# A third wait ahead of the GpSimd scatters of a two-layer graph network on one Trainium2 core

## The chip, the core and the metric

The kernel runs on one core of one Trainium2 chip. The metric is the device time of one execution in microseconds, the median of three runs.

## What is computed

The input is a graph of 6250 nodes with 128 features and 100000 edges, sorted by `dst`. Two layers follow each other, each ended by a residual addition and a layer norm:

```python
# layer 0
h = silu(concat(x[src], x[dst], radial(edge_weight)) @ Wm1 + bm1)
h = silu(h @ Wm2 + bm2);  messages = h @ Wm3 + bm3
out = segment_sum(messages, dst)
u = silu(concat(x, out) @ Wu1 + bu1) @ Wu2 + bu2
x = layernorm(x + silu(u @ Wi1 + bi1) @ Wi2 + bi2)
# layer 1, with xt = logmap0(x)
att = sigmoid(concat(xt[src], xt[dst], edge_attr) @ att_w + att_b)
agg  = segment_sum(xt[src] * att, src)
mean_src = segment_sum(edge_attr, src) / count(src)
mean_dst = segment_sum(edge_attr, dst) / count(dst)
x = layernorm(x + proj(expmap0(xt + agg + mean_src + mean_dst)))
```

`edge_attr` is 100000 rows of 128 floats. Summing its rows by `dst` is easy, since the edges come in that order; summing them by `src` needs them moved, and that is what the changed line is about.

## The kernel before

The edges are cut into M = 196 chunks of 512 edges (four tiles of 128). Five engines run their own instruction streams, written out tick by tick, and meet through semaphores. A stream is in order: an instruction that waits holds everything behind it on its engine.

**Edges of layer 0** (ticks -6 to 203). For each chunk GpSimd (POOL) issues four indirect gathers of projected node rows (L1060), which may run at most six chunks ahead of TensorE (`h1p`). TensorE turns them and multiplies (L1284 to L1324), ScalarE applies SiLU, VectorE builds one-hot matrices and adds each chunk's sum into an accumulator. All 784 gathers stand in POOL's stream ahead of the first scatter.

**Rows of layer 1** (row tick r = t - 190, so they overlap the last edges). Row chunk i passes these steps, with `row` a ring of NE = 8 slots:

- SyncE (SP) loads 512 edge rows into slot i % 8 (`row_load`, L893 to L896), three ticks before use. It first waits until the scatters of chunk i-8 have landed (`sc`) and until TensorE has summed chunk i-8 (`rp`).
- VectorE builds the window one-hot `od2` (L978) and the products for the attention (L981 to L996); ScalarE sums them into one more column of the slot (L944, or L949 and L952) and raises `lb`.
- One tick later TensorE sums the chunk by `dst` into a window of 78 nodes: four float matmuls, which are eight rows of the profile (`rows_pe`, L1010). The last raises `rp`, so `rp` counts the chunks summed. VectorE adds the window to `acce` (L970).
- POOL scatters the slot's rows to a table in HBM, grouped by `src` (`rows_pool`, L928 to L935): four indirect DMAs per chunk. It waits for the chunk's index (`idx`) and for `lb`.

SP's stream at a row tick r is: load of row chunk r+3, then for the later chunks the three look-up loads of chunk r+4 (L1428), then the loads of the units (below) of tick r+2 (L1414). All stand behind the wait of the row load.

**Units of layer 1** (row ticks 68 to 201). The table is read back in 189 units of up to six tiles (L1414), and each is summed by `src` with one-hot matmuls (VectorE L1534, TensorE L1651, VectorE L1557 or L1559). The edges are split in five groups (chunks 0 to 61, 62 to 112, 113 to 151, 152 to 178, 179 to 195); units of a group are loaded only when all scatters of the group have landed. Units 0 to 48 also need an attention sum on ScalarE (L1476). Units 172 to 188 belong to the last group, which ends with the last scatter.

After row tick 199 TensorE transposes the sums by `dst` (L1639), ScalarE scales them (L1483), the last units follow, and VectorE and ScalarE finish the nodes.

Of the kernel before, what the change touches and what calls it, by code (L numbers as in the profile page):

```python
# [7 lines left out]
M = 196  # L8
# [18 lines left out]
CAP = [q[1] * P for q in GROUPS]  # L27
FILL = 4
NCST = 264
STAGE = 9400  # L30


# [4 lines left out]
def group_of(m):  # L37
    return next(i for i in range(NG) if m <= LAST[i])
# [39 lines left out]
def limits():  # L78

    low = [2 * P * sum(1 for k in NDONE[:-2] if k <= m) for m in range(M)]  # L80
    high = [FREE - W if m < NFREE else 2 * EARLY * P - W if m < NEARLY else TOP for m in range(M)]
    return low, high
# [107 lines left out]
def gnn_kernel(nc, A, out):  # L190
# [10 lines left out]
    with ctx:  # L201

        def sb(name, shape, dt=f32):
            return ctx.enter_context(nc.sbuf_tensor(name, shape, dt))
# [7 lines left out]
        def take(reg, shape, dt=f32):  # L212
            n = 1
            for k in shape:
                n *= k
            return reg.take(shape, None if dt == f32 else dt, n // 2 if dt == bf16 else n)

        s = {n: ctx.enter_context(nc.semaphore(n)) for n in PRO + LAYER + NODES + ROWS + REST}
# [10 lines left out]

        cst = sb("cst", [P, NCST])  # L230
        ident, iota = cst[:, 0:128], cst[:, 128:256]
# [65 lines left out]
        sp1 = take(ring, [1])  # L297
        ring.off = STAGE
        stq = [take(ring, [4, H]) for _ in range(13)]
# [26 lines left out]
        def prologue_sp(e):  # L326
# [18 lines left out]
            for q in range(13):  # L345
# [4 lines left out]
                if q == 0:  # L350
                    SP.dma_start(lims.rearrange("o a m -> o (a m)"), A["consts"][0:1, NCST:NCST + 2 * M]).then_inc(s["lim"], 16)
                    e.wait_ge(s["c1"], 5)
# [29 lines left out]
        def prologue_act(e):  # L382
            S.dma_start(cst[:, :], A["consts"][:, 0:NCST]).then_inc(s["cst"], 16)
            e.wait_ge(s["z0"], 1)
            S.copy(sp1[:, 0:1], zerof[:, 0:1])
            for j in range(2):
                S.dma_start(x_sb[:, 12 * j:12 * j + 12, :], A["x"][12 * j * P:(12 * j + 12) * P, :].rearrange(
                    "(b p) f -> p b f", p=P)).then_inc(s[f"pt{j}"], 16)
            for t in range(14):
                q = t  # L390
                if q < 13:
                    nq = min(4, NB - 4 * q)
                    e.wait_ge(s["xt"], q + 1)
                    S.copy(xT[:, 4 * q * P:(4 * q + nq) * P], banks[5 + q % 2][:, 0:nq * P]).then_inc(s["xtc"], 1)
                q = t - 1
                if q >= 0:
                    nq = min(4, NB - 4 * q)
                    e.wait_ge(s["pp"], q + 1)
                    S.copy(stp[q][:, 0:nq, :].rearrange("p i f -> p (i f)"), banks[(0, 7)[q % 2]][:, 0:nq * P]).then_inc(s["pv"], 1)
            for q in range(13):  # L400
                nq = min(4, NB - 4 * q)
                e.wait_ge(s["qp"], q + 1)
                S.copy(stq[q][:, 0:nq, :].rearrange("p i f -> p (i f)"), banks[1 + q % 4][:, 0:nq * P]).then_inc(s["qv"], 1)
# [311 lines left out]
        rest0 = ring.off  # L715
        assert 13 * 4 * H + 8 * M + 1 <= rest0 <= STAGE
        od2 = [take(ring, [4, W]) for _ in range(NO2)]
        prod = [take(ring, [4, H + W]) for _ in range(NPR)]
        bwin = [take(ring, [W]) for _ in range(NWN)]
        row = [take(ring, [4, RC]) for _ in range(NE)]  # L720
        assert ring.off >= STAGE + 13 * 4 * H
        pat = take(ring, [FILL * RC])
# [204 lines left out]
        def rows_pool(e, i):  # L927
            e.wait_ge(s["idx"], i + 1)  # L928
            e.wait_ge(s["idxe"], 4)
            e.wait_ge(s["zf"], 16 * len(FILLS))  # L930
            e.wait_ge(s["lb"], i + 1)
            for n in range(4):
                G.indirect_dma_start(  # L933
                    out=gtab[group_of(i)][:, :], out_offset=bass.IndirectOffsetOnAxis(ap=idx[:, n, i:i + 1], axis=0),
                    in_=row[i % NE][:, n, :], in_offset=None).then_inc(s[f"sc{i % NE}"], 16)  # L935
# [112 lines left out]
        def layer_pool(e):  # L1048
            e.wait_ge(s["tp"], 13 * 16)
            e.wait_ge(s["r2"], 3)  # L1050
            e.wait_ge(s["b3"], 48)
            e.wait_ge(s["rb"], 1)
            e.wait_ge(s["c1"], 5)
            e.wait_ge(s["r3"], 5)
            for t in TICKS:
                i = chunk(t, 0)
                if i is not None:
                    e.wait_ge(s["h1p"], i + 1 - NGP)
                    for n in range(4):
                        G.indirect_dma_start(  # L1060
                            out=gp[i % NGP][:, n, :], out_offset=None, in_=ptab[:, :],
                            in_offset=bass.IndirectOffsetOnAxis(ap=gis[:, n, i:i + 1], axis=0)).then_inc(s[f"gp{i % NGP}"], 16)
            for i in range(RE):
                rows_pool(e, i)
# [392 lines left out]
        def rest_pool(e):  # L1457
            for i in range(RE, M):
                rows_pool(e, i)
# [614 lines left out]
def consts():  # L2074

    import numpy as np
    c = np.zeros((128, NCST + 2 * M), np.float32)
    p = np.arange(128)
# [12 lines left out]
    c[:, 263] = 1.0  # L2091
    c[0, NCST:] = np.array(limits(), np.float32).ravel()
    return c
# [18 lines left out]
```

## Time and profile before

| what | value |
|---|---|
| median of the runs | 2124.54 us (2124.5 to 2126.67, 3 runs) |
| profiled execution, first to last instruction | 2669.9 us |
| busy: PE, DVE, ACT, POOL | 66%, 63%, 51%, 56% of that span |
| gathers L1060 and scatters L933 on POOL | 784 each |
| first gather, first scatter, last scatter | 32.6, 1237.3, 2546.1 us |

The profiled execution is one execution with the profiler on; no other time of it is given than its span. The timed runs carry no profiler and are 545 us shorter. PE is TensorE's matmuls, DVE is VectorE, ACT is ScalarE, POOL is GpSimd, SP is SyncE. Idle time with the releaser "issue" is time in which the profile shows nothing that the engine waited for.

### The profile page before, as it was taken

How to read it: one execution, taken by the hardware profiler on the slowest of the kernel's cores; microseconds unless marked ns; L12 is line 12 of the kernel's file. 1: busy time of each engine (PE TensorE's matmuls, PEld its weight loads, DVE VectorE, ACT ScalarE, POOL GpSimd, SP SyncE). 2: the span in 40 equal slices, each digit the busy share in tenths (PEclk: the TensorE clock that was granted, in tenths of full speed). 3: DMA queues.
4: the chain of work that ended last, by engine and by line, in shares of the span. 5: the costliest groups of instructions: out<-in, count | busy, mean ns of one | idle time of the engine just before them, and what ended most of it. 6: DMA issues, size and time to landing. Idle time of an engine off the chain costs nothing.

```text
span 2669.9 us, 41647 instructions
## 1 busy us (share of the span) xinstructions
PE 1766.1 (66%) x11127; PEld 1530.4 (57%) x11127; DVE 1679.0 (63%) x5490; ACT 1361.0 (51%) x3965; POOL 1498.9 (56%) x1572
## 2 busy tenths in 40 slices
PE   5677777777878787776643244777775666576770
PEld 5466665655666666565533233677665656576660
DVE  5666666666666677776535334788765555466668
ACT  3666665665666666875425333666643233233224
POOL 3566666665666666655566665566555455555510
PEclk8788888898888778997755556677777677777795
DMA  7465655654333233333433335566555455455541
GB/s 192 122 148 124 150 131 130 148 133 111 88 84 86 84 86 85 87 83 103 133 89 100 87 105 140 160 187 186 171 155 151 147 154 152 142 168 167 172 136 49
DMA packets 337140, 341.98 MB, mean 128 GB/s; under 512 B 67402, under 2 KB 266948, under 8 KB 336898
## 3 DMA queue, kind: packets, MB, share of 16 engines
q1 hardware_dynamic: 283474, 233.47, 33.7%
q0 software_dynamic: 50176, 104.07, 13.2%
q10 hardware_dynamic: 3248, 1.71, 0.3%
q8 instruction: 93, 1.52, 0.2%
q14 instruction: 149, 1.22, 0.1%
HBM read 246.14 MB, written 90.15 MB: 126 GB/s over the span
## 4 chain that ended last, share of the span: by engine, by line
PE 30%; DVE 20%; issue 17%; another core or an unknown queue 15%; ACT 11%; DVEq 3%; SPq 0%; DMA 0%; ACTq 0%
PE bank L1651 8%; PE bank L1010 5%; PE bank L1630 4%; PE bank L1311 3%; DVEq L758 3%; PE bank L1284 3%; PE bank L1324 3%; DVE rt L987 2%; ACT L1093 2%; ACT L779 2%; ACT ring L1093 1%; PE bank L1320 1%; DVE ring L1184 1%; DVE ring L978 1%
## 5 line engine op out<-in xcount | busy, mean ns | idle before, releaser
L933 POOL DMA_INDIRECT gtab<-ring,idx x784 | 753.9, 962 | 556.3 <-ACT ring L952 238.9
L1060 POOL DMA_INDIRECT ra<-ptab,gis x784 | 744.9, 950 | 491.6 <-issue 199.7
L1010 PE MATMUL bank<-ring 128*128 128x78 f32 x1568 | 299.9, 341 | 284.0 <-issue 220.9
L949 ACT ACTIVATE rt<-rt 128x254 f32<-128x254 f32 x536 | 215.4, 403 | 470.7 <-DVE rt L989 347.6
L1010 PEld LDWEIGHTS bank<-ring 128*128 128x128 f32 x1568 | 278.0, 258 | 306.6 <-issue 251.0
L1284 PEld LDWEIGHTS bank<-ring 128*128 128x128 f32 x1568 | 232.9, 215 | 175.9 <-issue 153.8
L1073 ACT ACTIVATE ring<-bank 128x512 f32<-128x512 f32 x196 | 116.3, 594 | 395.3 <-remote 349.0
L1284 PE MATMUL bank<-ring 128*128 128x78 f32 x1568 | 238.1, 293 | 103.4 <-issue 86.4
L1651 PE MATMUL bank<-ring 128*128 128x130 f32 x1312 | 230.7, 332 | 86.5 <-issue 67.2
L1630 PE MATMUL bank<-rt 128*128 128x126 f32 x1072 | 196.6, 328 | 108.0 <-issue 73.8
L1311 PEld LDWEIGHTS bank<-wm,ring 128*128 128x128 f32 x1568 | 250.7, 228 | 25.5 <-issue 10.9
L1651 PEld LDWEIGHTS bank<-ring 128*128 128x128 f32 x1312 | 207.0, 238 | 100.5 <-issue 79.8
L1311 PE MATMUL bank<-wm,ring 128*128 128x128 f32 x1568 | 256.7, 316 | 11.5 <-issue 7.6
L1630 PEld LDWEIGHTS bank<-rt 128*128 128x128 f32 x1072 | 175.9, 240 | 114.1 <-issue 113.9
L1169 DVE TENSOR_TENSOR ra<-ra,bank 128x78 f32 x196 | 46.4, 237 | 234.3 <-issue 107.4
L1559 DVE TENSOR_TENSOR ra<-ra,bank 128x130 f32<-128x130 f32 (+2 forms) x140 | 47.4, 339 | 198.8 <-remote 156.4
L1324 PE MATMUL bank<-ra,ring 128*128 128x512 f32 x264 | 164.2, 709 | 7.5 <-issue 5.1
L944 ACT ACTIVATE ring<-ring 128x206 f32<-128x206 f32 x248 | 90.2, 366 | 149.2 <-issue 81.2
L1320 PE MATMUL bank<-cst,ra 128*128 128x128 f32 x784 | 147.7, 316 | 17.5 <-issue 17.3
L987 DVE SCALAR_TENSOR_TENSOR rt<-cst,rt,bank 128x125 f32<-128x125 f32 x536 | 147.7, 339 | 0.0
L1093 ACT ACTIVATE ring<-bank,bcol 128x512 f32<-128x512 f32 x196 | 134.6, 687 | 19.1 <-remote 15.1
L970 DVE TENSOR_TENSOR ra<-ra,bank 128x78 f32 x196 | 45.7, 233 | 152.4 <-remote 79.7
(274 smaller groups left out, 3817.3 us busy)
## 6 DMA issues: line engine op xcount, KB each, us to landing
ring<-in_edge_attr SPq DMA_DIRECT2D x196, 256.0 KB
ring<-gtab SPq DMA_DIRECT2D x89, 393.0 KB
gtab<-ring SPq DMA_DIRECT2D x36, 687.8 KB
ra<-in_edge_weight SPq DMA_DIRECT2D x132, 128.0 KB
ring<-gtab SPq DMA_DIRECT2D x49, 327.5 KB
ring<-reld SPq DMA_DIRECT2D x196, 78.0 KB
ring<-gtab SPq DMA_DIRECT2D x49, 262.0 KB
ra<-ptab,gis POOLq DMA_INDIRECT x784
```

Source lines behind the costliest of these rows:

```text
L933: G.indirect_dma_start(out=gtab[group_of(i)][:, :], out_offset=bass.IndirectOffsetOnAxis(ap=idx[:, n, i:i + 1], axis=0), in_=row[i % NE][: ...
L949: k = S.activation(prl[i % NPR][:, n, :], prl[i % NPR][:, n, :], ACT.Identity, accum_out=lgs[i % 2][:, n:n + 1])
L987: V.scalar_tensor_tensor(out=v[:, n, H:H + NM], in0=iota[:, 0:NM], scalar=srcm[:, n, i:i + 1], in1=bk[:, n, 0:NM], op0=ALU.is_equal, op1=A ...
L1010: k = T.matmul(bk[:, 256:256 + W], row[i % NE][:, n, 0:H], od2[i % NO2][:, n, :], start=(first and n == 0), stop=(n == 3), skip_group_chec ...
L1060: G.indirect_dma_start(out=gp[i % NGP][:, n, :], out_offset=None, in_=ptab[:, :], in_offset=bass.IndirectOffsetOnAxis(ap=gis[:, n, i:i + 1 ...
L1093: S.activation(h1[i % 2], banks[(1, 5)[i % 2]][:, :], ACT.Silu, bias=bcol[:, 3:4]).then_inc(s["h1"], 1)
L1284: k = T.matmul(small_bank(t)[:, 0:W], val[i % NVAL][:, n, :], ohd[i % NOD][:, n, :], start=(n == 0), stop=(n == 3), skip_group_check=True)
L1311: k = T.matmul(bk[:, n * P:(n + 1) * P], h1[i % 2][:, n * P:(n + 1) * P], wm2[:, :], start=False, stop=True, skip_group_check=True)
L1320: T.matmul(bk[:, n * P:(n + 1) * P], v[:, n, :], ident, start=(n == 0), stop=False, is_transpose=True, skip_group_check=True)
L1324: T.matmul(bk[:, :], qw[i % NQW], rad[i % NRD], start=False, stop=True, skip_group_check=True).then_inc(s["h1p"], 1)
L1630: k = T.matmul(banks[(1, 2)[i % 2]][:, n * P:n * P + NM + 1], lkf[i % 2][:, n * P:(n + 1) * P], tw[i % NLK][:, 0:NM + 1], start=(n == 0), ...
L1651: k = T.matmul(bk[:, j * (H + 2):(j + 1) * (H + 2)], coh1[(u - 4) % NCO][:, j * nk + n, :], ct[(u - 4) % NCT][:, j * nk + n, 0:H + 2], sta ...
```

## The change

POOL waits once more before the four scatters of chunk i: until TensorE has summed min(i + 3, 196) chunks, that is chunks i, i+1 and i+2. For chunks 194 and 195 the count was already waited for at chunk 193, so 194 of the 196 chunks get the new wait.

```diff
@@ -27,6 +27,7 @@
 FILL = 4
 NCST = 264
+AHEAD = 3
 STAGE = 9400
@@ -929,6 +930,7 @@
             e.wait_ge(s["idxe"], 4)
             e.wait_ge(s["zf"], 16 * len(FILLS))
             e.wait_ge(s["lb"], i + 1)
+            e.wait_ge(s["rp"], min(i + AHEAD, M))
             for n in range(4):
                 G.indirect_dma_start(
```

No instruction moves, on any engine; the line numbers behind the edits grow by one or two. POOL's stream, in the middle of the scatters, of the kernel before (the table's size stands behind its name, and x3 are three more of the same chunk):

```order
L933 DMA gtab<-ring,idx 51456x131 [waits lb,idx]
L933 DMA gtab<-ring,idx 51456x131 x3
L933 DMA gtab<-ring,idx 51456x131 [waits lb,idx]
L933 DMA gtab<-ring,idx 51456x131 x3
L933 DMA gtab<-ring,idx 51456x131 [waits lb,idx]
```

The same place in the changed kernel:

```order
L935 DMA gtab<-ring,idx 51456x131 [waits rp,lb,idx]
L935 DMA gtab<-ring,idx 51456x131 x3
L935 DMA gtab<-ring,idx 51456x131 [waits rp,lb,idx]
L935 DMA gtab<-ring,idx 51456x131 x3
L935 DMA gtab<-ring,idx 51456x131 [waits rp,lb,idx]
```

The first scatter of each chunk names a third semaphore, and nothing else differs.

## Rows read from the trace of the kernel before

**Rows 1.** The page's head and first part: the span, and busy us and shares of the engines

```profile
span 2669.9 us, 41647 instructions
PE 1766.1 (66%) x11127; PEld 1530.4 (57%) x11127; DVE 1679.0 (63%) x5490; ACT 1361.0 (51%) x3965; POOL 1498.9 (56%) x1572
```

**Rows 2.** The page's groups: busy us, mean ns of one, idle before and its releaser

```profile
L933 POOL DMA_INDIRECT gtab<-ring,idx x784 | 753.9, 962 | 556.3 <-ACT ring L952 238.9
L1060 POOL DMA_INDIRECT ra<-ptab,gis x784 | 744.9, 950 | 491.6 <-issue 199.7
```

**Rows 3.** POOL in order of time: start, us, what, idle before; first gathers, last scatters

```profile
32.55 1.11 POOL L1060 DMA_INDIRECT ra<-ptab,gis  x1 [32.10 <-DMA ptab<-ring]
...
81.28 0.99 POOL L1060 DMA_INDIRECT ra<-ptab,gis  x1 [18.32 <-PE bank L1324]
82.58 0.94 POOL L1060 DMA_INDIRECT ra<-ptab,gis  x1 [0.30 <-issue]
...
2531.47 0.96 POOL L933 DMA_INDIRECT gtab<-ring,idx  x1 [6.22 <-ACT ring L952]
...
2542.34 0.96 POOL L933 DMA_INDIRECT gtab<-ring,idx  x1 [0.30 <-issue]
...
2546.14 0.96 POOL L933 DMA_INDIRECT gtab<-ring,idx  x1 [0.30 <-issue]
```

**Rows 4.** PE in order of time, 2196 to 2209 us: single matmuls far apart

```profile
2198.91 0.36 PE L1651 MATMUL bank<-ring 128*128 128x130 f32 x1 [1.05 <-issue]
2200.33 0.27 PE L1651 MATMUL bank<-ring 128*128 128x130 f32 x1 [1.06 <-issue]
...
2208.99 1.85 PE L1010 MATMUL bank<-ring 128*128 128x78 f32 x8
```

**Rows 5.** Busy us (count) of PE, PEld, DVE, ACT, POOL in four stretches; clock, DMA

```profile
300.00:1000.00 700.00, 544.23 (x3568) 438.62 (x3568) 470.53 (x1620) 440.43 (x599) 435.65 (x460) 0.85 0.44 110
1242.40:1602.60 360.20, 152.30 (x732) 137.62 (x733) 154.29 (x513) 138.98 (x620) 222.78 (x232) 0.55 0.37 100
1694.00:1901.00 207.00, 149.02 (x900) 141.43 (x900) 165.59 (x453) 132.66 (x744) 124.24 (x130) 0.76 0.63 177
1954.00:2547.00 593.00, 399.55 (x2452) 374.00 (x2453) 335.07 (x982) 177.60 (x863) 319.47 (x332) 0.74 0.53 154
```

**Rows 6.** POOL in order of time: first scatters of chunks 40, 41, 43; last of 41

```profile
1491.88 0.96 POOL L933 DMA_INDIRECT gtab<-ring,idx  x1 [0.30 <-issue]
...
1499.49 0.96 POOL L933 DMA_INDIRECT gtab<-ring,idx  x1 [2.87 <-remote]
...
1503.28 0.96 POOL L933 DMA_INDIRECT gtab<-ring,idx  x1 [0.31 <-issue]
...
1509.59 0.96 POOL L933 DMA_INDIRECT gtab<-ring,idx  x1 [0.30 <-issue]
```

**Rows 7.** PE in order of time: sums by dst of chunks 42 and 45

```profile
1489.15 1.97 PE L1010 MATMUL bank<-ring 128*128 128x78 f32 x8 [0.77 <-issue]
...
1504.13 1.96 PE L1010 MATMUL bank<-ring 128*128 128x78 f32 x8 [0.43 <-issue]
```

**Rows 8.** SP in order of time: the row load of chunk 49

```profile
1508.31 0.38 SPq L896 DMA_DIRECT2D ring<-in_edge_attr  x1
```

**Rows 9.** DVE in order of time: one tick with a unit's attention, first groups of two ticks

```profile
1801.61 0.23 DVE L970 TENSOR_TENSOR ra<-ra,bank 128x78 f32 x1 [0.54 <-issue]
...
1806.69 0.23 DVE L970 TENSOR_TENSOR ra<-ra,bank 128x78 f32 x1
```

**Rows 10.** The tail, PE then DVE in order of time, and the chain's longest ACT piece

```profile
2541.38 1.01 PE L1010 MATMUL bank<-ring 128*128 128x78 f32 x8
...
2554.66 11.45 ACT ra L1483 x44
...
2570.99 0.95 DVE L1534 TENSOR_TENSOR gis<-bank,ring 128x768 f32<-128x768 f32 x1
```

**Rows 11.** The tail: SP's unit loads from 2567.88, and DVE's first use of that one

```profile
2567.88 4.40 SPq L1414 DMA_DIRECT2D ring<-gtab  x4
...
2573.40 0.95 DVE L1534 TENSOR_TENSOR ring<-bank,ring 128x768 f32<-128x768 f32 x1
```

## The prediction

> **What bounds the kernel now.** I read the page first, then the groups, then the engines in order of time. The page says that no engine is busy for more than 66% of 2669.9 us [rows 1], and that POOL's two groups have nearly the same price: 0.950 us per gather and 0.962 us per scatter, 784 of each [rows 2]. In order of time an indirect DMA is followed by the next after 0.30 us even where nothing is waited for [rows 3]. So a gather takes 1.25 us of POOL's stream and a scatter 1.262 us, and a chunk of four takes 5.0 or 5.05 us.
>
> Next the stretches [rows 5]. I divide by the chunks in each, POOL's count over four:
> - edges (115 chunks): PE 4.73, DVE 4.09, POOL 3.79 busy and 5.0 with its gaps, of 6.09 us;
> - stage A, rows alone (58 chunks): PE 2.63, DVE 2.66, ACT 2.40, POOL 5.05, of 6.21;
> - stage B, rows and units with attention (32.5 chunks): DVE 5.10, PE 4.59, ACT 4.08, POOL 5.05, of 6.37;
> - stage C, rows and plain units (83 chunks): PE 4.81, DVE 4.04, ACT 2.14, POOL 5.05, of 7.14.
>
> No sum per chunk reaches the stretch's own pace. What fills the difference is seen on PE: after a dense run come single matmuls 1.4 us apart, with idle time that nothing explains, until it is dense again [rows 4]. I take these to belong to the profiled execution, because the timed runs are 545 us shorter. Laying POOL's stream end to end gives a check: 32.55 us before the first gather, 784 x 1.25 = 980.0, the one long wait of 18.3 at the start, 784 x 1.262 = 989.4, and 2669.9 - 2547.1 = 122.8 after the last scatter [rows 1 to 3]. That is **2143 us, 0.9% above the median of 2124.54**. A kernel whose POOL stream alone adds up to its time has next to no idle POOL in the runs. So I read the runs as bound by POOL in the edges, in A and in C, and balanced between POOL (5.05) and DVE (5.10) in B.
>
> **The change, step by step.** The edit touches only POOL's stream. It adds a condition to 194 scatters and no DMA, load or matmul. The condition itself is priced at nothing: chunks already open with two waits, and the gap at such a scatter, 0.30 us where nothing is late, is the gap inside a chunk [rows 3, 6]. Held to both sides it costs 0 to 194 x 0.30 = 58 us (a whole gap for every wait). I take 0, since two waits show none, and give 58 us no part of the range: it would need a third wait to cost what two together do not.
>
> What the wait can cost is POOL idle until TensorE has summed chunk i+2.
> - *Where POOL is behind*, it costs nothing. The trace has such a place in A: chunk 40 is scattered from 1491.88, and the sum of chunk 42 ends at 1489.15 + 1.97 = 1491.12; chunk 43 goes at 1509.59, the sum of 45 ended at 1506.09, 3.5 us before [rows 6, 7]. With POOL the bound the ring of eight slots decides how far. The last scatter of chunk 41 leaves POOL at 1504.24 and the load into its slot is issued at 1508.31 [rows 6, 8], so a landing costs at most 4.1 us. From the first scatter of chunk i to the sum of i+8 I count 5.05 + 4.1, about 4 for the load and two to three for VectorE and TensorE: some 17 us. Chunk i+6 is scattered 30 us after chunk i, so the sum of i+8 is there 13 us early. The margin is **13 us**.
> - *Start.* POOL's gathers stand ahead of scatter 0, so the rows pipeline runs ahead of it up to the ring's eight slots. Scatters start a few chunks late with their sums made: 0 us.
> - *B.* DVE's tick is 1806.69 - 1801.61 = 5.08 us [rows 9], POOL's 5.05. POOL catches up by 0.03 us in each of 49 ticks, 1.5 us of the 13: 0 us.
> - *C.* DVE 4.04 against POOL 5.05: POOL falls behind again, 0 us.
> - *End.* In the profile POOL is not behind here. The sum of chunk 195 ends at 2541.38 + 1.01 = 2542.39; chunk 193's scatters began at 2531.47 and 195's at 2542.34 [rows 3, 10]. Now the twelve scatters of 193 to 195 all start after 2542.39, and the last ends 15.1 us later at 2557.5 instead of 2547.1: **10.4 us later**. Behind it wait the units of the last group. Their first use on VectorE is at 2570.99, because ScalarE's scaling of the sums by dst holds TensorE for 11.45 us [rows 10]. With 4.1 to land and 5.5 for the unit's load (2567.88 to 2573.40, the closest load and use in the tail [rows 11]), they are there at 2567.1. So it is covered; without that cover it is 10.4. In the runs, with POOL behind, the sums are done before and nothing is late.
>
> The sum is 0 us of POOL idle in the runs, and 0 to 4 on the profiled span of 2669.9 us, where covers are thinner. The time stays 2124.5.
>
> One rule speaks against the change. The row shows only that a landing costs up to 4.1 us past POOL's last scatter [rows 6, 8]. The Trainium skill, DMA: Bandwidth & Descriptors, Rules for kernel authors, says to issue a DMA early and wait for it late; here each scatter is issued later, up to 2.5 ticks. By the rule the deferral is lost time, the 12.7 us of rival 1 and a time of 2137; by the row it is lost only where POOL is not behind, and the sum stays 0. The same page, Anatomy of one DMA, puts a fixed cost of about 2.0 us on a DMA; by that, an estimate, the margin would be 15 us and the sum the same.
>
> **The rivals.**
> 1. *Slower: POOL catches up in B and then pays.* If a B tick in the runs is above 5.05 + 13/49 = 5.32 us, the margin is gone before B ends. The wait then opens holes that the old order filled, up to 2.5 ticks of 5.08, **12.7 us**, and C, being POOL's, never gives them back: up to 2137. For it: DVE's 5.08 has its own gap of 0.54 in front, and look-up loads are late now and then. Against it: TensorE's 4.59 and ScalarE's 4.08 leave DVE alone near the line [rows 5].
> 2. *Slower: SP is held in C.* SP waits for the scatters of chunk i before it issues the loads that stand behind (row, look-ups, units), and in a kernel not bound by POOL that closes a loop of four ticks: 5.05 + 4.1 after the sum of i+2, 5.5 for the loads, about 2.5 to the next sum, 17.2 us, so no tick under 4.3. Against DVE's 4.04 it would be 84 x 0.26 = 22 us, 2146. It needs a POOL faster than 4.3 us per chunk in the runs, against rows 2 and 3.
> 3. *Faster.* Scatters held back leave the DMA engines (busy share 0.53 to 0.63 in B and C [rows 5]) to the loads for a while. If the runs are waiting for loads rather than POOL, the price is at most rival 2's, the other way; I put it at half, 11 us, 2113. Nothing of it counts while POOL is the bound.
> 4. *The runs are like the profile*, POOL idle for a fifth of A to C. Then only the end changes, 0 to 4 us: up to 2128. It falls in "same".
>
> **How the numbers follow.** A measurement of this kernel can tell 0.2%, 4.2 us. Forecast, no POOL idle: 0.56, of which 0.02 for a wait that costs after all. Rival 4: 0.08. Rival 1: 0.22, of which 0.19 costs more than 4.2 us. Rival 2: 0.07. Rival 3: 0.07. Faster by over 0.2%: 0.07. Slower: 0.19 + 0.07 + 0.02 = 0.28. The rest, 0.65, within 0.2%. The time is the likeliest, 2124.5. The range takes in rival 1 whole (2137) and a little of rival 2, up to 2139, and of rival 3 a part, down to 2119; outside lie most of rivals 2 and 3, 0.12.
>
> **What would show it.** In the profile after, POOL's scatters name TensorE's L1010 as releaser, for a few hundred microseconds of idle time that was put down to ScalarE before, and the first scatter of a chunk stands right behind the third sum, in B and C some 12 us later than now. The last scatter starts about 10 us later against the last L1010. The groups' counts and mean durations stay. The span stays near 2670 us. Wrong would be: the median moved by over 4 us; a longer idle of VectorE in front of L1534 or L1525 with loads as releaser (rival 2); or a DVE tick in B above 5.3 us (rival 1).

## The result and the profile after

The kernel before takes 2124.5 us (2121.14 to 2126.67, 5 runs), the changed one **2132.41 us** (2131.18 to 2136.2, 5 runs): a ratio of 1.0039, 95% interval 1.0028 to 1.005, or 7.9 us slower. The prediction had 2124.5, no difference. The time lies in its range of 2119 to 2139, on the side that was given 0.28.

One thing must be known to read what follows. The experiments ran in sets, each of several kernels that run on one chip in turn with the kernel before, and every set fell in one of two conditions. In the **first condition** the kernel before takes 2120 to 2125 us. In the **second condition** all kernels of the set are longer, and the kernel before takes 2674 to 2703 us. The profile of before that the prediction read (2669.9 us) is of the second condition; its three timed runs and the result above are of the first. One chip showed both, in different sets. Each run below stands against the kernel before of its own set.

The page of the changed kernel, its head and its two POOL groups, against [rows 1, 2]:

```profile
span 2133.5 us, 41647 instructions
PE 1544.3 (72%) x11127; PEld 1322.7 (62%) x11127; DVE 1677.7 (79%) x5490; ACT 1360.0 (64%) x3965; POOL 1505.0 (71%) x1572
...
L1062 POOL DMA_INDIRECT ra<-ptab,gis x784 | 748.2, 954 | 272.5 <-issue 235.2
L935 POOL DMA_INDIRECT gtab<-ring,idx x784 | 756.6, 965 | 248.2 <-issue 220.0
```

POOL's busy time is that of before within 7 us, and its idle time in front of gathers and scatters is 521 us where it was 1048. Of the 521, 455 (235.2 and 220.0) are put down to "issue", the 0.30 us gaps. That is the reading that the forecast assumed for the runs: a stream of POOL with next to no holes. Before and after stand in different conditions here, so this fall isn't the effect of the change.

Four stretches of the changed kernel (busy us and count of PE, PEld, DVE, ACT, POOL; then clock, DMA share, GB/s), one in each of the prediction's stages: edges, A, B, C, against [rows 5]:

```profile
300.00:1000.00 700.00, 580.85 (x4384) 461.96 (x4384) 587.47 (x2113) 562.10 (x823) 530.25 (x557) 0.97 0.49 124
1100.00:1330.00 230.00, 98.12 (x414) 89.08 (x414) 114.51 (x367) 96.90 (x483) 174.57 (x183) 0.51 0.41 117
1366.00:1568.00 202.00, 142.19 (x1109) 129.81 (x1108) 199.05 (x553) 162.33 (x912) 153.34 (x160) 1.00 0.83 225
1609.00:1956.00 347.00, 268.95 (x2004) 260.13 (x2004) 275.77 (x813) 142.28 (x684) 264.14 (x273) 0.89 0.78 220
```

By POOL's count over four these are 139.25, 45.75, 40 and 68.25 chunks, so 5.03, 5.03, 5.05 and 5.08 us per chunk, where the prediction had 6.09 to 7.14 from [rows 5]. In every stretch the pace is POOL's. In B, VectorE is busy for 199 of 202 us: balanced, as predicted.

POOL in order of time (start, us, what, idle before and its releaser), against [rows 3, 6]: the first gather, the first scatters of chunks 0 to 6, of 40 (and the last of it), of 193, and the last of all. Of the later gathers only the one at 64.83 us is idle for over 0.5 us before it, for 1.92:

```profile
32.46 1.11 POOL L1062 DMA_INDIRECT ra<-ptab,gis  x1 [32.01 <-DMA ptab<-ring]
...
1021.41 0.99 POOL L935 DMA_INDIRECT gtab<-ring,idx  x1 [0.30 <-issue]
...
1026.77 0.96 POOL L935 DMA_INDIRECT gtab<-ring,idx  x1 [0.56 <-issue]
...
1033.73 0.96 POOL L935 DMA_INDIRECT gtab<-ring,idx  x1 [2.20 <-PE bank L1012]
...
1041.94 0.96 POOL L935 DMA_INDIRECT gtab<-ring,idx  x1 [3.47 <-PE bank L1012]
...
1048.88 0.96 POOL L935 DMA_INDIRECT gtab<-ring,idx  x1 [2.17 <-PE bank L1012]
...
1055.10 0.96 POOL L935 DMA_INDIRECT gtab<-ring,idx  x1 [1.46 <-PE bank L1012]
...
1061.10 0.96 POOL L935 DMA_INDIRECT gtab<-ring,idx  x1 [1.25 <-PE bank L1012]
...
1233.77 0.96 POOL L935 DMA_INDIRECT gtab<-ring,idx  x1 [0.30 <-issue]
...
1237.57 0.96 POOL L935 DMA_INDIRECT gtab<-ring,idx  x1 [0.30 <-issue]
...
2011.01 0.96 POOL L935 DMA_INDIRECT gtab<-ring,idx  x1 [0.30 <-issue]
...
2024.92 0.96 POOL L935 DMA_INDIRECT gtab<-ring,idx  x1 [0.30 <-issue]
```

Over the plain gap of 0.30 the six idle times are 0.26 + 1.90 + 3.17 + 1.87 + 1.16 + 0.95 = **9.3 us**, and of the other scatters none waits over 0.5 us. Laid end to end: 32.5 before the first gather, 989.0 to the first scatter, 1004.5 to the end of the last, 107.6 behind it, 2133.5 us; without the 9.3 it is 2124.2, near the time of before. It can't be taken as nearer than a few us: the profiled execution is the longest of the five (2136.2 us), and its span is 2.7 us shorter than its time. The sums by dst on TensorE say why POOL waits. Chunks 2 to 8, then 42 and 195:

```profile
1016.78 1.12 PE L1012 MATMUL bank<-ring 128*128 128x78 f32 x8 [2.36 <-DVE ring L980]
...
1024.87 1.12 PE L1012 MATMUL bank<-ring 128*128 128x78 f32 x8 [1.22 <-DVE ring L980]
...
1031.82 1.12 PE L1012 MATMUL bank<-ring 128*128 128x78 f32 x8 [1.32 <-DVE ring L980]
...
1039.16 2.00 PE L1012 MATMUL bank<-ring 128*128 128x78 f32 x8 [2.34 <-DVE ring L980]
...
1046.97 1.12 PE L1012 MATMUL bank<-ring 128*128 128x78 f32 x8
...
1053.19 1.12 PE L1012 MATMUL bank<-ring 128*128 128x78 f32 x8 [1.42 <-DVE ring L980]
...
1059.20 1.12 PE L1012 MATMUL bank<-ring 128*128 128x78 f32 x8 [0.97 <-DVE ring L980]
...
1213.23 1.97 PE L1012 MATMUL bank<-ring 128*128 128x78 f32 x8 [3.01 <-DMA ring<-in_edge_attr]
...
2004.32 1.01 PE L1012 MATMUL bank<-ring 128*128 128x78 f32 x8
```

The seven sums from 1016.78 to 1059.20 start one every 7.1 us, while POOL asks for one in 5.06. In this stretch both engines have the last edges to do as well: TensorE is busy for 34.83 of the 42.40 us, VectorE for 31.73, and before six of the sums TensorE waits for VectorE. The next two sums end at 1064.28 and 1068.95 us, each 4 to 5 us after the one before. When the first scatter could go, at 1021.4, three sums were made. Against a POOL that went on at 5.06 us, each later one was further behind until chunk 8. This lateness is called the debt below.

### The profile page after: what moved, and what is told of

It is laid out like the page before. It is cut to its first block, busy times and chain, and to the rows that moved or that the text cites. A ratio compares the mean times of both kernels' runs of the same rounds, so it can differ in the third digit from the quotient of the medians.

```text
span 2133.5 us, 41647 instructions
## 1 busy us (share of the span) xinstructions
PE 1544.3 (72%) x11127; PEld 1322.7 (62%) x11127; DVE 1677.7 (79%) x5490; ACT 1360.0 (64%) x3965; POOL 1505.0 (71%) x1572
## 4 chain that ended last, share of the span: by engine, by line
DVE 34%; POOL 25%; issue 15%; DMA 8%; PE 7%; DVEq 7%; ACT 2%; SPq 1%; POOLq 0%; ACTq 0%
POOL gtab L935 16%; POOL ra L1062 10%; DVEq L759 6%; DVE ring L1186 4%; DVE ring L1196 3%; DMA gtab<-ring,idx 3%; DVE ring L1201 2%; PE bank L1653 2%; DVE bank L1210 2%; DVE rt L989 2%; DMA ring<-btab 2%; DMA rt<-bval 2%; DVE ring L1191 2%; DVE ring L1207 2%; DVE ring L1188 2%
## 5 line engine op out<-in xcount | busy, mean ns | idle before, releaser
L1062 POOL DMA_INDIRECT ra<-ptab,gis x784 | 748.2, 954 | 272.5 <-issue 235.2
L1012 PE MATMUL bank<-ring 128*128 128x78 f32 x1568 | 260.2, 323 | 133.3 <-DMA ring<-in_edge_attr 94.4
L1012 PEld LDWEIGHTS bank<-ring 128*128 128x128 f32 x1568 | 246.3, 239 | 144.3 <-issue 116.3
L1286 PEld LDWEIGHTS bank<-ring 128*128 128x128 f32 x1568 | 198.8, 195 | 147.2 <-DVE ra L1171 129.0
L1286 PE MATMUL bank<-ring 128*128 128x78 f32 x1568 | 210.5, 278 | 67.1 <-DVE ring L1178 61.6
L1632 PE MATMUL bank<-rt 128*128 128x126 f32 x1072 | 167.1, 305 | 105.4 <-DVE rt L991 91.1
L1653 PE MATMUL bank<-ring 128*128 128x130 f32 x1312 | 183.9, 292 | 56.8 <-DVE ra L1561 43.1
L1313 PEld LDWEIGHTS bank<-wm,ring 128*128 128x128 f32 x1568 | 215.5, 200 | 12.4 <-ACT ring L1095 6.4
L1632 PEld LDWEIGHTS bank<-rt 128*128 128x128 f32 x1072 | 149.3, 215 | 118.1 <-issue 117.9
L1313 PE MATMUL bank<-wm,ring 128*128 128x128 f32 x1568 | 217.6, 284 | 4.9 <-ACT ring L1095 4.9
L1653 PEld LDWEIGHTS bank<-ring 128*128 128x128 f32 x1312 | 165.4, 200 | 66.1 <-DVE ra L1561 47.6
L1171 DVE TENSOR_TENSOR ra<-ra,bank 128x78 f32 x196 | 46.4, 237 | 130.1 <-issue 121.9
L1527 DVE TENSOR_SCALAR rt<-rt,cst 128x512 f32<-128x512 bf16 x134 | 67.5, 504 | 102.0 <-DMA rt<-bval 101.1
L1322 PEld LDWEIGHTS bank<-cst,ra 128*128 128x128 f32 x784 | 95.0, 148 | 62.9 <-DMA ra<-ptab,gis 62.8
```

Of the source, the lines that this page charges most:

```text
L1012: k = T.matmul(bk[:, 256:256 + W], row[i % NE][:, n, 0:H], od2[i % NO2][:, n, :], start=(first and n == 0), stop=(n == 3), skip_group_chec ...
L1062: G.indirect_dma_start(out=gp[i % NGP][:, n, :], out_offset=None, in_=ptab[:, :], in_offset=bass.IndirectOffsetOnAxis(ap=gis[:, n, i:i + 1 ...
L1286: k = T.matmul(small_bank(t)[:, 0:W], val[i % NVAL][:, n, :], ohd[i % NOD][:, n, :], start=(n == 0), stop=(n == 3), skip_group_check=True)
L1313: k = T.matmul(bk[:, n * P:(n + 1) * P], h1[i % 2][:, n * P:(n + 1) * P], wm2[:, :], start=False, stop=True, skip_group_check=True)
L1322: T.matmul(bk[:, n * P:(n + 1) * P], v[:, n, :], ident, start=(n == 0), stop=False, is_transpose=True, skip_group_check=True)
L1632: k = T.matmul(banks[(1, 2)[i % 2]][:, n * P:n * P + NM + 1], lkf[i % 2][:, n * P:(n + 1) * P], tw[i % NLK][:, 0:NM + 1], start=(n == 0), ...
```

## The experiments

Theory (the start theory of the expectations): the whole cost is this debt at the start. Rivals: a cost at every chunk (of the third wait itself, or of loads that come later in B and C), and a cost at the end. The first set also has the kernel before again.

**e1, the wait at chunks 7 and later alone.**

```diff
-            e.wait_ge(s["rp"], min(i + AHEAD, M))
+            if i >= 7:
+                e.wait_ge(s["rp"], min(i + AHEAD, M))
```

> The new wait stands only at chunks 7 and later; chunks 0 to 6 keep the two old waits. Theory (the start pays): the profile of the changed kernel shows POOL idle over its 0.30 us gap only at the scatters of chunks 1 to 6, together 9.3 us; without the wait there, the time is that of the kernel before, 2124.5 us (2121 to 2127), and POOL's scatters of chunks 0 to 6 follow each other every 5.05 us. Rival (the wait costs a little at every chunk, by its own execution or by loads that come later in B and C): the cost is spread over 196 chunks, 189 of them are left, so 2132 us. Rival (half and half, the pipeline downstream loses elsewhere what it gains at the start): between 2127 and 2130.

**e2, the wait at chunks 0 to 6 alone** (`if i < 7:`).

> The new wait stands only at chunks 0 to 6. Theory (the start pays): the whole cost is there, 2132.4 us (2130 to 2135), with POOL idle some 9 us over its gaps at chunks 1 to 6 released by TensorE's bank. Rival (the wait costs at every chunk): the time of the kernel before, 2124.5 us.

**e3, one chunk ahead** (`AHEAD = 2`).

> The scatters of chunk i wait for the sum by dst of chunk i+1 instead of i+2. From the ends of the sums in the profile of the changed kernel (1010.6, 1017.9, 1026.0, 1032.9, 1041.2, 1048.1, 1054.3, 1060.3 for chunks 1 to 8) and a first scatter at 1021.4 with 5.06 us a chunk, chunk i waits for: chunk 1 at 1026.5 none, 2 at 1031.5 until 1032.9 (1.4 us), 3 at 1038.0 until 1041.2 (3.2), 4 at 1046.3 until 1048.1 (1.8), 5 at 1053.2 until 1054.3 (1.1), 6 at 1059.4 until 1060.3 (0.9), 8.4 us, if the sums do not come earlier when the scatters do. That is nearly the cost of the changed kernel, 2124.5 + 8.4 x 0.85 = 2131.6 us. Should the sums come earlier because the scatters do (the unit and row loads stand behind them), the cost is less, about 2 us: 2126.5. Rival (a cost at every chunk whatever it waits for): 2132.4.

**e4, the kernel before, unchanged.**

> The kernel before, unchanged, for a profile of it near the time of its runs. Theory: the span is near 2125 us, not 2670; TensorE has no matmuls 1.4 us apart; POOL has no idle time over its 0.30 us gap at the scatters of chunks 1 to 6, and the sums of chunks 2 to 8 end after the scatters of chunks 0 to 6 begin. Rival (the single matmuls belong to the kernel before and the change has removed them): a span near 2670 us again.

Measured in that set: the kernel before 2702.74 us (2682.73 to 2720.06, 17 runs); e1 2598.93, ratio 0.9603 (0.9558 to 0.9647); e2 2702.33, ratio 0.9994 (0.9963 to 1.0026); e3 2579.31, ratio 0.9536 (0.9492 to 0.958); e4 2690.46. No expectation was made for this condition, and only the span of e4's rival fits (2687.6 us, near 2670 again). Its reason, that the change had removed the single matmuls, doesn't: e3 has the wait, and its TensorE is still idle for 169.2 us in front of L1012 with the releaser "issue". Two things follow. The single matmuls far apart [rows 4] do not belong to a profiled execution, as I had written: here all 17 runs of the kernel before take even longer than that profile. And the wait from chunk 7 on, which costs 0.3% in the first condition (e7 below), takes 4% off in the second (e1). The changed kernel itself was not run in the second.

**e5, the changed kernel again, and e6, three chunks ahead** (`AHEAD = 4`), in one set.

> The changed kernel itself, beside the one before, in the same call as the next run. The first four runs of this study fell on a chip where the kernel before takes 2703 us, TensorE has its single matmuls 0.7 to 1.4 us apart in the profile, and the wait at chunks 7 and later alone took the time down to 2599 us (ratio 0.960), while the wait at chunks 0 to 6 alone left it (0.999). Theory: there are two conditions of the chip with two answers. Where the kernel before takes some 2700 us, the changed kernel takes 2600 us, as with the late wait alone (2590 to 2610). Where it takes 2124, the changed kernel takes 2132. Rival: the 2124 and 2132 of the first result were two different days and the change is faster on every chip: a ratio of 0.96 with a time near 2040.

> The scatters of chunk i wait for the sum by dst of chunk i+3. Where the kernel before takes 2124 us (start theory): from the ends of the sums in the profile of the changed kernel, scatter 0 waits for 1026.0 and scatter 6 for 1064.3, 13 to 15 us at the start; in B the margin of 5.2 us less a tick of 5.06 is nothing and in C 2 to 7 us less 5 costs 0 to 40 us more: 2138 to 2180. The rival that only the start pays: 2138 to 2140. Where it takes 2700 us: the time between the sum of i+3 and the load of the row i+8 closes a loop of five ticks instead of six, about 22 us for scatter, landing, load and sum, 4.4 us per tick against the 6.2 us that the stretches keep there, so no cost: 2590 to 2610.

This set fell in the first condition: before 2121.8 us, e5 2130.03, ratio 1.0034 (1.0021 to 1.0048), 8.2 us, so the result stands. e6 took 2172.53, ratio 1.0254 (1.0236 to 1.0272), 50.7 us, inside the 2138 to 2180 of the margins and not the 2138 to 2140 of a start that alone pays. The waits view of e6 from 1360 us on, in stages B and C (waited for: us in total, times, longest):

```profile
POOL gtab L935 <- PE bank L1012: 38.8, 37, 3.8
```

One more chunk uses up what margin there was in B and C. Over the plain gaps e6's POOL is idle for 49.9 us, and 11.7 of them lie before 1060 us, so some 38 of the 50.7 are lost in B and C.

**e7 to e9 repeat e1 to e3, and e10 is four chunks ahead** (`AHEAD = 5`).

> The new wait at chunks 7 and later alone, again, meant for the condition in which the kernel before takes 2122 us. Start theory: nothing is left of the cost, 2122 (2119 to 2125). Rival (a cost at every chunk): 2130. Where it falls on a chip like that of the first four runs: 2599 against 2703 as before, and the question stays as it was.

> The new wait at chunks 0 to 6 alone, again, meant for the same condition. Start theory: the whole cost, 2130 (2128 to 2133). Rival (a cost at every chunk): 2122.

> One chunk ahead instead of two, again, meant for the same condition. By the ends of the sums in the changed kernel 8.4 us of POOL idle at chunks 2 to 6, and 2129; if the sums come earlier when the scatters do, because row loads stand behind them, about 2 us and 2124.

> The scatters of chunk i wait for the sum of chunk i+4. Three chunks ahead (scatter i behind the sum of i+3) cost 50.7 us over the kernel before, of which the start was put at 13 to 15. Loop theory: scatter i lets the row load of i+8 go (POOL's four scatters 5.06, landing 2 to 3.6, load 4, VectorE and TensorE 2 to 3, 14 to 17 us in all), and scatter i+4 waits for the sum of i+8: a loop over four chunks with 14 to 17 us plus the wait of SP in order, so a tick of 3.7 to 4.3 us by itself, but 5.06 is POOL's; the cost comes from the look-up and unit loads that stand ahead of the row load on SP. From 50.7 at three chunks ahead I expect the margin to be short by another tick in B and C, where the sum came 2 to 7 us before it was asked for at two ahead: another 5 us once and then a tick longer than POOL's, 5.6 to 7.5 us in B and C (131 chunks): 2250 to 2500. Start-only rival: 2143.

The kernel before took 2124.19 us (18 runs); e7 2129.5, ratio 1.0031 (1.0019 to 1.0043); e8 2130.73, 1.003 (1.0019 to 1.0041); e9 2125.24, 1.0005 (0.9996 to 1.0014); e10 2359.24, 1.1108 (1.1093 to 1.1123).

e8 came as expected (2128 to 2133). e7 is a miss: 5.3 us where I expected none. POOL in order of time in e7, the first scatters of chunks 7 and 9:

```profile
1063.07 0.96 POOL L936 DMA_INDIRECT gtab<-ring,idx  x1 [6.24 <-PE bank L1013]
...
1074.13 0.96 POOL L936 DMA_INDIRECT gtab<-ring,idx  x1 [1.25 <-PE bank L1013]
```

The first seven chunks went at POOL's pace, and the debt was asked for whole at chunk 7. So the cost is not a sum over the chunks that wait but about the largest lateness among them: with e8's 6.5 us it would make 11.8, and both waits together cost 8.2 (e5). My cut at 7 was too early for the test.

e9 shows the same from the other side. POOL in order of time, first scatters of chunks 5 to 7:

```profile
1047.81 0.96 POOL L935 DMA_INDIRECT gtab<-ring,idx  x1 [1.32 <-PE bank L1012]
...
1054.12 0.96 POOL L935 DMA_INDIRECT gtab<-ring,idx  x1 [1.52 <-PE bank L1012]
...
1060.12 0.96 POOL L935 DMA_INDIRECT gtab<-ring,idx  x1 [1.26 <-PE bank L1012]
```

One chunk less is 5.06 us of debt less: 3.2 us of idle time over the gaps, and 1.05 on the time, not to be told from none. The 8.4 us that I expected of e9 had set each scatter against a sum one chunk too far on. In all these kernels the time grows by less than POOL's idle time over the gaps: 7.9 for 9.3 us in the changed kernel, 6.5 for 8.0 in e8, 5.3 for 7.6 in e7. No run shows where the 1 to 2 us between them go. e10 fell in the range of the loop theory, 235 us slower. Its waits views, whole run, for POOL and VectorE:

```profile
POOL gtab L935 <- PE bank L1012: 251.2, 101, 8.7
```

```profile
DVE rt L1527 <- DMA rt<-bval: 308.9, 112, 10.1
```

The same wait of VectorE in the changed kernel:

```profile
DVE rt L1527 <- DMA rt<-bval: 101.1, 71, 9.3
```

VectorE waits three times as long for a look-up load, which SP issues behind its wait for the scatters.

**e11 and e13, the wait at chunks 20 and later alone** (`if i >= 20:`), **e12 and e14, a third wait that is met long before**, at every chunk:

```diff
-            e.wait_ge(s["rp"], min(i + AHEAD, M))
+            e.wait_ge(s["rp"], max(i - NE + 1, 1))
```

> The new wait at chunks 20 and later alone. With the wait at 7 and later the time was 2129.5 against 2124.2, and its profile shows POOL idle for 6.24 us at chunk 7 and 1.25 at chunk 9: the debt of the start was paid there, because the sum of chunk 9 was still 7 us late against scatters that follow each other every 5.06 us. From chunk 19 on the sum of i+2 ends 17 us before the scatters of i ask for it in every profile of this condition. Start theory, in its new form (the cost is the largest lateness of a sum over all chunks that wait): nothing, 2124 (2122 to 2126). Rival (a wait costs something in B, C or at the end too): at most 1.0 us was seen at chunk 189, 2125; over that, 2127 to 2129, if what was lost at chunk 7 was not the cause.

> A third wait at all 196 chunks' scatters, but for the sum of chunk i-7 (of chunk 0 at the first ones), which is there long before: the price of the condition alone. Step priced at 0: 2124 (2122 to 2126), and a gap of 0.30 us before each scatter as inside a chunk. Upper end of the range that was written down: 0.30 us for each of 196, 2183. If a met wait costs 10 ns, 2126.

The set fell in the second condition (before 2673.86 us): e11 2568.45, ratio 0.9593 (0.9549 to 0.9637); e12 2673.96, 1.0008 (0.9979 to 1.0037). Both were taken again, with the wait in **C alone** (`if i >= 113:`) and in **A and B alone** (`if 20 <= i < 113:`).

> The wait at chunks 20 and later alone, again. Where the kernel before takes 2124 us: start theory 2124 (2122 to 2126); rival (the wait costs in B, C or at the end) 2127 to 2130. Where it takes 2700: 0.96 of it, as before.

> A third wait at every chunk that is met long before, again: the ratio was 1.0008 [0.9979, 1.0037] where the kernel before took 2674 us. Where it takes 2124: 1.000 (2122 to 2126).

> The wait at chunks 113 and later alone (stage C). Where the kernel before takes 2124 us: 2124; if C or the end costs anything by itself, 2126 to 2129. Where it takes 2700: the profiles of that condition have 7.3 us per chunk in C without the wait and 6.25 with it, so 82 x 1.05 = 86 us, but POOL is also 20 us ahead of TensorE when C begins: 70 to 86 us of the 105 to 120, ratio 0.968 to 0.974. Rival (the gain needs the wait in A and B): 1.00.

> The wait at chunks 20 to 112 alone (A and B). Where the kernel before takes 2124 us: 2124. Where it takes 2700: what is left of the gain, 20 to 40 us, ratio 0.985 to 0.993; the rival has the whole gain, 0.96.

First condition, before 2120.45 us (33 runs): e13 2121.25, ratio **1.0005** (0.9996 to 1.0014); e14 2120.97, 1.0002 (0.9993 to 1.0011); e15 2120.43, 1.0 (0.9991 to 1.0009); e16 2120.96, 1.0002 (0.9993 to 1.0011). A met wait costs nothing that these runs can tell (at most 2.3 us by the interval), and neither does this one from chunk 20 on, in A, B, C or at the end (at most 3.0 us, e13). What is left is the start. In e13's waits view of the whole run there is still TensorE as POOL's releaser, but no wait is longer than the gap:

```profile
POOL gtab L936 <- PE bank L1013: 10.4, 34, 0.3
```

e14 also shows the debt as it lies in the order of before. POOL, first scatters of chunks 0, 6 and 8, then TensorE's sum of chunk 8:

```profile
1017.66 0.98 POOL L935 DMA_INDIRECT gtab<-ring,idx  x1 [0.30 <-issue]
...
1048.01 0.96 POOL L935 DMA_INDIRECT gtab<-ring,idx  x1 [0.30 <-DVE idx L1212]
...
1059.25 0.96 POOL L935 DMA_INDIRECT gtab<-ring,idx  x1 [1.27 <-ACT ring L946]
```

```profile
1055.64 1.12 PE L1012 MATMUL bank<-ring 128*128 128x78 f32 x8 [0.97 <-DVE ring L980]
```

The sum of chunk 8 ends at 1056.76, **8.75 us** after chunk 6 was scattered. From a sum's end to the scatter that it releases e7 has 0.78 us (1061.23 + 1.06 to 1063.07). That makes 9.5, less the 0.97 us over the gap that POOL waits at chunk 8 here for ScalarE, which a later stream would not meet: 8.6 us, against 7.9 and 8.2 measured. That is the largest of four: the first scatter comes earliest in e14 (1017.66 us, in the others 1019.6 to 1021.8). In the profiles of e13, e15 and e16, which have no wait at the start either, the sum of chunk 8 ends 6.2, 4.6 and 6.3 us after chunk 6 is scattered, which makes 5.4 to 7.1 with the 0.78. The debt has the size of the cost, within 3 us.

**e17 and e18 repeat e15 and e16.**

> The wait in C alone, meant for the condition in which the kernel before takes 2700 us: ratio 0.968 to 0.974, C at 6.3 us a chunk instead of 7.3. Rival (the gain needs the wait in A and B): 1.00. Where the kernel before takes 2124: 1.000 again.

> The wait in A and B alone, the same: ratio 0.985 to 0.993, C at 7.3 us a chunk; the rival has 0.96. Where the kernel before takes 2124: 1.000 again.

This set fell in the second condition, before 2679.56 us: C alone 2578.1, ratio 0.9628 (0.958 to 0.9675), A and B alone 2657.17, 0.9937 (0.9901 to 0.9974). C holds nearly the whole gain, even a little more than I gave it. What changes is seen on TensorE in C, 1990 to 2380 us. First e17, the windows row (its columns as above) and TensorE's longest waits. "Issue" is again idle time for which the profile shows no reason:

```profile
1990.00:2380.00 390.00, 278.04 (x1851) 265.06 (x1852) 253.85 (x757) 130.71 (x627) 243.19 (x252) 0.80 0.63 181
```

```profile
PE bank L1654 <- issue: 31.4, 26, 6.2
PE bank L1013 <- issue: 26.1, 32, 1.2
PE bank L1654 <- DVE ra L1562: 25.0, 9, 8.6
PE bank L1633 <- issue: 14.4, 18, 1.8
```

The same of e18, which has no wait in C:

```profile
1990.00:2380.00 390.00, 251.48 (x1534) 233.97 (x1534) 211.86 (x630) 109.06 (x523) 201.06 (x209) 0.72 0.52 149
```

```profile
PE bank L1654 <- issue: 70.1, 55, 5.3
PE bank L1013 <- issue: 39.1, 52, 1.8
PE bank L1654 <- DVE ra L1562: 16.6, 7, 4.6
PE bank L1633 <- issue: 11.6, 19, 1.2
```

With the wait: 63 chunks in 390 us, 6.19 each, of which 71.9 / 63 = 1.14 are such idle time. Without it: 52.25 chunks, 7.46 each, with 120.8 / 52.25 = 2.31. A chunk gains 1.27 us, and on TensorE these are made up so: **1.17 us less** idle time without a visible cause, 0.40 less busy time (4.81 to 4.41, at a granted clock of 0.72 and 0.80), and 0.30 more of the other waits, nearly all for VectorE. In the first condition C has none of the first in this view: e15 from 1610 to 1940 us needs 5.06 us a chunk, at a granted clock of 0.92, and its longest wait is for VectorE:

```profile
1610.00:1940.00 330.00, 246.60 (x1898) 236.79 (x1897) 262.50 (x777) 136.13 (x654) 250.45 (x261) 0.92 0.78 221
```

```profile
PE bank L1654 <- DVE ra L1562: 55.7, 29, 4.0
```

What TensorE stalls on there, and why it stalls less when scatters are held back, stays open. No run here changes that alone. The DMA engines aren't ruled out: over 40 slices of this stretch their traffic swings between 49 and 268 GB/s in e18 and between 146 and 215 in e17.

## Why the prediction was wrong

- **Bound.** Right for the runs: POOL's stream end to end, 5.03 to 5.08 us a chunk in all four stretches of the profile after. The argument for it was right (the sum over POOL's stream against the median), but its 0.9% had luck in it: of the pieces taken from the other condition, the long wait of the gathers is 1.9 us here and not 18.3, and the end behind the last scatter 107.6 and not 122.8, while gathers and scatters take more than the sum gave them. The reason given for the gap between profile and runs was wrong: not the profiled execution but a condition that lasts for a whole set of runs. The sign that was named, a few hundred us of POOL put down to TensorE, did not come either: the changed kernel's scatters wait for L1012 for 24.3 us in all.
- **The wait's own price, 0.** Right: e14, 1.0002 (0.9993 to 1.0011). The upper end of 58 us was rightly given no part.
- **Where POOL is behind, a margin of 13 us.** Right in sign, larger in A and smaller later. Its own terms add to 15 to 16 us and not to 17, which makes 14 to 15. Chunk 40 is scattered at 1233.77 and the sum of 42 ended at 1215.20: 18.6 us. Laid side by side over the whole profile after, the two streams have a margin of 4.1 to 6.1 us in B and of 2.0 to 8.5 in C, so one more chunk ahead, 5 us, brings 37 waits there (e6). The landing, put at 4.1 at most, is 1.9 us at chunk 40: its last scatter leaves POOL at 1238.53, and SP in order of time has

```profile
1240.38 0.38 SPq L897 DMA_DIRECT2D ring<-in_edge_attr  x1
```

- **Start, 0 us. This is the step that failed.** I wrote that the rows pipeline runs ahead up to the ring's eight slots, and that "scatters start a few chunks late with their sums made". The ring lets eight rows be loaded, not summed. At the first scatter three sums were made (chunks 0 to 2), and the next came 7.1 us apart, because the rows share TensorE and VectorE with the last edges. POOL needs 5.05. The step should have read 9.3 us of POOL idle and some 8 on the time. The rows for it were to be had: the ends of the sums of the first ten chunks beside POOL's first forty scatters. I took the margin from a place in the middle of A and argued the start in words.
- **B, 0.** Right: two ticks of VectorE in the changed kernel are 5.08 us apart, as in [rows 9], and the wait in A and B alone, from chunk 20 on, costs nothing (e16).

```profile
1400.54 0.23 DVE L972 TENSOR_TENSOR ra<-ra,bank 128x78 f32 x1
...
1405.62 0.23 DVE L972 TENSOR_TENSOR ra<-ra,bank 128x78 f32 x1
```

- **C and End, 0.** Right for the runs (e15). The last sum ends at 2005.33, before chunk 193 is scattered at 2011.01, so the 10.4 us of [rows 10] never arise, as was said for a POOL that is behind. The cover that I named is gone, though: after the last scatter, which ends at 2025.88, VectorE waits for the unit's load (SP and VectorE in order of time, against [rows 11]), so a scatter that came later would, by this reading, be paid. No run tests it.

```profile
2027.58 21.54 SPq L1416 DMA_DIRECT2D ring<-gtab  x16
```

```profile
2032.57 0.96 DVE L1536 TENSOR_TENSOR gis<-bank,ring 128x768 f32<-128x768 f32 x1 [3.98 <-DMA ring<-gtab]
```

- **Rival 1** (POOL catches up in B, then pays up to 12.7 us) had the mechanism, a debt paid once and never given back, at the wrong place. The Trainium skill, DMA: Bandwidth & Descriptors, Rules for kernel authors (issue early, wait late) spoke against the change. The trace agrees where the sums were late, at the start (9.3 us of POOL idle), and not from chunk 20 on, where POOL was behind and the deferral cost nothing (e13).
- **Rival 2**, the loop over SP, needs more than this change waits for: two chunks more have it (e10, 235 us, and VectorE's wait for look-up loads at 309 us instead of 101), one chunk more has the beginning of it (e6, 134 us).
- **Rival 3** (faster, 11 us) has the sign of the second condition, where the late waits take 100 us off, but its size is far off, and whether its mechanism is the one isn't shown: what goes is TensorE's own idle time.
- **Rival 4** (runs like the profile, and then only the end changes, 0 to 4 us) was wrong: in the second condition, which is that of the profile, the wait in C alone takes 101 us off (e17).

## What to carry to other kernels

A wait for work some chunks ahead, on the engine that bounds the kernel, cost about the largest lateness that it met, once, and neither the sum nor the mean: lay the two streams side by side at the start, where the pipeline fills and shares its engines with the stage before, and not only in the middle. A ring that is full of loads says nothing of how many of them have been worked on. If such a wait is wanted, let it begin where the debt has been paid: from chunk 20 on it cost nothing in one condition (1.0005) and took 4.1% off in the other (0.9593), so in no set was it behind the kernel before by more than the noise, and one chunk ahead at every chunk (1.0005 and 0.9536) did as well.

## What the runs showed of the hardware

The same program has two conditions that are 26 to 27% apart, 2120 to 2125 and 2674 to 2703 us (medians of the kernel before), each for all runs of a set, and both on one chip (the sets of e1 and of e5). In the longer one the kernel before has a granted clock of 0.76 instead of 0.88 over the span. TensorE's busy time per chunk in C goes with the clock: 3.78, 4.41 and 4.81 us at 0.92, 0.80 and 0.72 (e15, e17, e18). But the clock is not all: in e17's and e18's C TensorE is idle without a reason in the profile for 1.14 and 2.31 us a chunk, and in e15's for none. So a profile that is a quarter longer than its runs isn't to be put down to profiling here. Every share, tick and margin in it belongs to another condition, and the wait from chunk 7 on had the opposite sign there (0.9603 against 1.0031).

Two POOL scatters that wait for nothing stay 0.30 us apart whether a chunk opens with two waits or with three, as long as they are met (e14).
